# Joining the user tiles two weight blocks later in an embedding-mean projection

## The chip, the cores and the metric

The kernel runs on one core of one Trainium2 chip. The metric is the device time of one execution in microseconds (us). The profile is of one execution, and its times count from the start of its span.

## The reference

There are 1024 users with 200 ids each, a table of 12500 rows of 512 floats, and a projection of 512 by 12500 with a bias.

```
valid = sequence_ids < emb_table.shape[0]
seq_emb = emb_table[where(valid, ids, 0)] * valid
user_repr = seq_emb.sum(axis=1) / max(valid.sum(axis=1), 1)
logits = user_repr @ proj_w + proj_b
```

The ids are drawn up to 109962, so only about one in nine is valid. The kernel sorts each user's ids so that the valid ones stand first, and gathers the first 26 of them (FAST), one "column" of 128 rows at a time. Users that have more get a share called the rest.

## The kernel before

**Tiles and units.** The users are 8 tiles of 128. The projection's 12500 outputs are 25 blocks of 500 (BW). A *unit* is one tile times one block. In fp32 precision it takes 12 matmuls on TensorE (PE), four for each of high*high, high*low and low*high. There are 200 units, and a unit's number is `r`. While ScalarE (ACT) moves a unit out of PSUM (`by_act`), the bias is a thirteenth matmul (line 806). Where VectorE (DVE) moves it out (line 609), the bias is part of the move. Until unit `joined[1]` ACT moves all units, until `joined[5]` every second one (the even `r`), then DVE moves all.

**Weights.** A *load* q brings block q modulo 25 (1000 KB) by a DMA of the queue SP, line 283. ACT copies it to `w_hi` (line 416, `w_high`), DVE forms `w_lo` (lines 595 and 597, `w_low`). The split blocks stand in a ring of 5 (SPLIT). The raw loads stand in a ring of 4 up to load 15, since two buffers lie over the means of tiles 4 to 7, which are written later (`raw_at_hi`, `raw_at_lo`). From load 16 on (MORE_LOADS) the ring has the 2 buffers `w_raw`. SP asks for a load once `w_low` is done with the load that had its buffer before:

```
raw_slot = [q if q <= ONCE else (q - 1) % ONCE if q < MORE_LOADS else q % RAW for q in range(LOADS)]
split_due = [None] * SPLIT + [min(last_unit[q - SPLIT] + 1, first_unit[q] - 1) for q in range(SPLIT, LOADS)]
```

`split_due[q]` is the unit at which ACT and DVE split load q in their program order. ACT waits there for the load, and what stands behind it on ACT waits too.

**Means and joins.** The sum of a tile's 26 columns must be there before the tile's first unit, the tile's *join*. GpSimd (POOL) gathers the columns (line 347) into a ring of 12 (ROWS): gather c needs column c-11 to be used (c even). DVE adds most columns into `sums` (line 539). PE adds the last 8 of tile 1 and the last 2 of tile 2 into `turned` by diagonal matrices (line 757) that ACT builds (line 400, `diagonal`, a ring of 4). The steps of a join are: the rest's share (PE line 749, ACT line 433), the mean (DVE line 584), the turn (PE line 732), `mean_hi` (ACT line 422), `mean_lo` (DVE line 589). Between two joins DVE also sorts the next tile's ids (lines 478 to 496). I call the stretch from the turn of tile t-1 to the turn of tile t *stage t*.

**What sets the order.** The tuple JOIN gives the load at which each tile joins. A tile joins with the last four loads still in the ring of 5 and then takes part in each load for 25 blocks. From JOIN all lists above are computed at build time (`units`, `first_unit`, `last_unit`, `joined`, `split_due`, `column_due`), and each engine's program is one loop over `r` in which these lists say what stands where. DVE's columns of tile t are spread evenly from unit `joined[t-1] - 2` (0 for tile 1) to unit `joined[t] - 3`.

```
JOIN=(0, 10, 14, 17, 20, 22, 24, 26)
start = [max(0, q - (SPLIT - 1)) if t else 0 for t, q in enumerate(JOIN)]
```

On ACT, in the loop over `r`, the diagonals stand ahead of `w_high(q)` of the same `r`, and behind those of the units before:

```
for c in range(FAST, COLS):
    if by_pe[c] and column_due(c) == r + 1:
        diagonal(c)
for q in range(SPLIT, LOADS):
    if split_due[q] == r:
        w_high(q)
if by_act[r]:
    move_out(r)
```

Of the kernel before, what the change touches and what calls it, by code (L numbers as in the profile page):

```python
# [3 lines left out]


def mean_embedding_projection(nc, ids, table, proj, bias, out, FAST=26,
                              JOIN=(0, 10, 14, 17, 20, 22, 24, 26)):
    F32, F32R, BF16 = mybir.dt.float32, mybir.dt.float32r, mybir.dt.bfloat16
    I32, U32 = mybir.dt.int32, mybir.dt.uint32
    ALU, ACT, AX = mybir.AluOpType, mybir.ActivationFunctionType, mybir.AxisListType  # L10
# [38 lines left out]

    start = [max(0, q - (SPLIT - 1)) if t else 0 for t, q in enumerate(JOIN)]  # L50
    LOADS = start[-1] + NB
    steps = []
    for q in range(LOADS):
        for t in range(1, TILES):
            if JOIN[t] == q:
                steps += [(x, t, 1) for x in range(start[t], q)]
        here = [t for t in range(TILES) if JOIN[t] <= q < start[t] + NB]
        steps.append((q, here[0], len(here)))
# [41 lines left out]
    raw_last = [max((x for x in range(q) if raw_slot[x] == raw_slot[q]), default=None) for q in range(LOADS)]  # L100
    assert MORE_LOADS < JOIN[TILES // 2] and RAW_AT + BW <= (STAGE - K) * BW

# [728 lines left out]
```

## Time and profile before

| | |
|---|---|
| median of 3 executions | 642.86 us (642.55 to 642.87) |
| the profiled execution | 643.35 us |
| its span | 641.6 us |
| PE busy | 609.1 us (95%) |
| DVE busy | 407.9 us (64%) |
| POOL busy | 233.6 us (36%) |
| ACT busy | 137.6 us (21%) |
| joins (first unit of tiles 1 to 7) | 10, 22, 35, 51, 65, 81, 98 |
| loads | 47 |

PE is busy nearly throughout, so what counts is each gap on PE and what ended it. A busy share of another engine is to be read by stage: DVE has 64% over the span, but the means are all formed in the first 357 us.

### The profile page before, as it was taken

How to read it: one execution, taken by the hardware profiler on the slowest of the kernel's cores; microseconds unless marked ns; L12 is line 12 of the kernel's file. 1: busy time of each engine (PE TensorE's matmuls, PEld its weight loads, DVE VectorE, ACT ScalarE, POOL GpSimd, SP SyncE). 2: the span in 40 equal slices, each digit the busy share in tenths (PEclk: the TensorE clock that was granted, in tenths of full speed). 3: DMA queues.
4: the chain of work that ended last, by engine and by line, in shares of the span. 5: the costliest groups of instructions: out<-in, count | busy, mean ns of one | idle time of the engine just before them, and what ended most of it. 6: DMA issues, size and time to landing. Idle time of an engine off the chain costs nothing.

```text
span 641.6 us, 7583 instructions
## 1 busy us (share of the span) xinstructions
PE 609.1 (95%) x2602; PEld 476.1 (74%) x2602; DVE 407.9 (64%) x723; ACT 137.6 (21%) x153; POOL 233.6 (36%) x227
## 2 busy tenths in 40 slices
PE   1878799989999999999999999999999999999997
PEld 0326558777778787788788788888888888888886
DVE  7977958989878898697786454333333333344442
ACT  7605426132122131300200221110011111211210
POOL 5777777777764767566550000000000000000000
PEclk9999989999999999999999999999999999999999
DMA  9979999999998999798793398454555555566632
GB/s 311 388 259 331 380 390 293 373 329 318 315 296 298 305 291 313 236 323 249 236 341 121 97 288 260 127 173 161 177 176 177 176 177 176 171 185 201 223 127 103
DMA packets 77703, 158.31 MB, mean 247 GB/s; under 512 B 9287, under 2 KB 65042, under 8 KB 77658
## 3 DMA queue, kind: packets, MB, share of 16 engines
q1 hardware_dynamic: 60378, 110.30, 50.7%
q0 software_dynamic: 17280, 47.47, 23.2%
q8 instruction: 21, 0.34, 0.2%
q14 instruction: 24, 0.20, 0.1%
HBM read 115.70 MB, written 51.20 MB: 260 GB/s over the span
## 4 chain that ended last, share of the span: by engine, by line
PE 75%; DVE 13%; DMA 6%; issue 5%; ACT 1%; DVEq 1%; POOL 0%; POOLq 0%; ACTq 0%
PE acc L801 70%; DVE sums L539 5%; DMA rows<-in_L_rec_emb_table_dram,index 4%; PE turned L757 2%; DMA w_raw<-in_L_rec_proj_w_dram 2%; DVE w_lo L597 2%; DVE key L496 1%; DVE w_lo L595 1%; DVE top L492 1%; PE acc L806 1%; ACT w_hi L416 1%; DVE stage L609 1%; PE turned L749 1%; DVE mean L584 0%; PE turned L732 0%
## 5 line engine op out<-in xcount | busy, mean ns | idle before, releaser
L347 POOL DMA_INDIRECT rows<-in_L_rec_emb_table_dram,index x208 | 224.1, 1077 | 95.7 <-issue 58.1
L801 PE MATMUL acc<-w_hi,mean_hi 128*128 128x500 f32 x800 | 224.4, 402 | 0.8 <-ACT mean_hi L422 0.8
L609 DVE TENSOR_TENSOR stage<-acc,bias_sb 128x500 f32<-128x500 f32 x162 | 109.3, 676 | 179.4 <-PE acc L801 179.3
L801 PE MATMUL acc<-w_hi,mean_lo 128*128 128x500 f32 x800 | 213.8, 389 | 0.3 <-DVE mean_lo L589 0.3
L801 PE MATMUL acc<-w_lo,mean_hi 128*128 128x500 f32 x800 | 214.0, 389 | 0.0
L801 PEld LDWEIGHTS acc<-w_hi,mean_lo 128*128 128x128 f32 x800 | 150.1, 188 | 32.4 <-DVE mean_lo L589 1.6
L801 PEld LDWEIGHTS acc<-w_hi,mean_hi 128*128 128x128 f32 x800 | 150.2, 189 | 31.9 <-issue 4.3
L801 PEld LDWEIGHTS acc<-w_lo,mean_hi 128*128 128x128 f32 x800 | 150.2, 188 | 31.3
L539 DVE SCALAR_TENSOR_TENSOR sums<-rows,mask,sums 128x512 f32<-128x512 f32 x165 | 124.1, 752 | 8.8 <-DMA rows<-in_L_rec_emb_table_dram,index 0.6
L416 ACT ACTIVATE w_hi<-w_raw 128x2000 fp32r<-128x2000 f32 x39 | 72.9, 1875 | 236.3 <-PE acc L801 215.7
L595 DVE TENSOR_TENSOR w_lo<-w_raw,w_hi 128x1000 fp32r<-128x1000 f32 x39 | 46.5, 1193 | 13.4 <-ACT w_hi L416 13.3
L597 DVE TENSOR_TENSOR w_lo<-w_raw,w_hi 128x1000 fp32r<-128x1000 f32 x39 | 46.6, 1196 | 0.0
L407 ACT ACTIVATE stage<-acc 128x500 f32<-128x500 f32 x38 | 22.2, 586 | 79.9 <-PE acc L806 79.9
L433 ACT ACTIVATE rest_mean<-turned,inv_count 128x512 f32<-128x512 f32 x7 | 4.8, 690 | 76.3 <-PE turned L749 68.9
L757 PE MATMUL turned<-rows,diags_at_hi 128*128 128x512 f32 x30 | 15.8, 663 | 3.1 <-DMA rows<-in_L_rec_emb_table_dram,index 3.1
L492 DVE MAX8 top<-key 128x8 f32<-128x200 f32 x40 | 14.6, 366 | 0.7
L757 PEld LDWEIGHTS turned<-rows,diags_at_hi 128*128 128x128 f32 x30 | 5.8, 210 | 12.4 <-DMA rows<-in_L_rec_emb_table_dram,index 7.2
L757 PE MATMUL turned<-rows,diag 128*128 128x512 f32 x20 | 11.2, 698 | 3.9 <-ACT diag L400 3.7
L806 PE MATMUL acc<-bias_parts,pick 89*128 89x500 bf16 x38 | 14.6, 385 | 0.0
L422 ACT ACTIVATE mean_hi<-turned 128x512 fp32r<-128x512 f32 x8 | 4.8, 598 | 45.4 <-PE turned L732 45.4
L584 DVE SCALAR_TENSOR_TENSOR mean<-sums,inv_count,rest_mean 128x512 f32<-128x512 f32 x7 | 5.3, 751 | 14.0 <-issue 6.9
L496 DVE MATCH_REPLACE8 key<-top,key 128x200 f32<-128x200 f32 x40 | 14.1, 352 | 0.0
(106 smaller groups left out, 180.9 us busy)
## 6 DMA issues: line engine op xcount, KB each, us to landing
out_dram<-stage SPq DMA_DIRECT2D x200, 250.0 KB, 3.8
w_raw<-in_L_rec_proj_w_dram SPq DMA_DIRECT2D x39, 1000.0 KB, 6.6
bias_sb<-in_L_rec_proj_b_dram SPq DMA_DIRECT2D x39, 250.0 KB, 4.9
raw_at_hi<-in_L_rec_proj_w_dram SPq DMA_DIRECT2D x4, 1000.0 KB, 11.1
rows<-in_L_rec_emb_table_dram,index POOLq DMA_INDIRECT x208, 5.8
raw_at_lo<-in_L_rec_proj_w_dram SPq DMA_DIRECT2D x3, 1000.0 KB, 13.7
stage<-in_L_rec_proj_w_dram SPq DMA_DIRECT2D x1, 1000.0 KB, 23.8
ids_sb<-in_r_sequence_ids_dram SPq DMA_DIRECT2D x1, 700.0 KB, 4.4
```

The source lines that it names most:

```text
L347: return pool.indirect_dma_start(out=dst, out_offset=None, in_=table, in_offset=bass.IndirectOffsetOnAxis(ap=column, axis=0), bounds_check ...
L407: nc.scalar.activation(stage[:, g % STAGE, r - stores[g][0]], acc[:, r % BANKS, 0:BW], ACT.Copy).then_inc(s_moved_by_act, 1)
L416: nc.scalar.activation(w_hi[:, q % SPLIT], raw(q), ACT.Copy).then_inc(s_w_hi, 1)
L492: dve.max(eight, key[:]).then_inc(s_sort, 1)
L496: dve.match_replace(key[:], eight, key[:], -1.0).then_inc(s_sort, 1)
L539: dve.scalar_tensor_tensor(sums[:], rows[:, c % ROWS], mask[:, t, j:j + 1], sums[:], ALU.mult, ALU.add).then_inc(s_summed, 1)
L595: dve.tensor_tensor(w_lo[:, q % SPLIT, 0:half], raw(q)[:, 0:half], w_hi[:, q % SPLIT, 0:half].bitcast(F32), ALU.subtract)
L597: dve.tensor_tensor(w_lo[:, q % SPLIT, half:], raw(q)[:, half:], w_hi[:, q % SPLIT, half:].bitcast(F32), ALU.subtract).then_inc(s_w_lo, 1)
L609: dve.tensor_tensor(stage[:, g % STAGE, r - stores[g][0]], acc[:, r % BANKS, 0:BW], bias_sb[:, i % BIAS], ALU.add).then_inc(s_moved_by_dve, 1)
L757: nc.tensor.matmul(turned[:], diagonal_of(c), rows[:, c % ROWS], start=j == 0, stop=j == FAST - 1).then_inc(s_added, 1)
L801: last = nc.tensor.matmul(bank, first, second, start=part + k == 0, stop=part == 2 and k == K - 1 and not by_act[r])
L806: last = nc.tensor.matmul(bank, pick[:, q % NB:q % NB + 1].to_broadcast([BIAS_ROWS, P]), bias_parts[:], start=False, stop=True)
```

## The change

Every tile from the second on joins two loads later. The kernel's text changes in one line:

```
-                              JOIN=(0, 10, 14, 17, 20, 22, 24, 26)):
+                              JOIN=(0, 12, 16, 19, 22, 24, 26, 28)):
```

Worked out from the lists: tile 0 takes 12 loads alone instead of 10. The joins stand at units 12, 24, 37, 53, 67, 82 and 98. There are 49 loads instead of 47, and still 200 units. ACT moves out 40 units instead of 38, so two more bias matmuls run. From unit 98 on each unit's place in the program is the same, with each load's number two higher. MORE_LOADS stays at 16, ON_PE (which columns PE adds) stays as it is. In stage 3 the loads split are 17, 18 and 19 (at units 25, 26, 27) instead of 15, 16 and 17 (at 23, 24, 25). In stage 2 they are 13 to 16 instead of 11 to 14. Ahead of tile 1's join, up to the unit before the diagonals, they run to load 12 instead of load 10.

**ScalarE ahead of the join of tile 1.** The rows are of the difference on ACT, from the split of load 10 on; `raw_at_hi` and `raw_at_lo` are loads 11 and 12.

```order
 L416 ACTIVATE w_hi<-w_raw 128x2000
 L407 ACTIVATE stage<-acc 128x500
+L416 ACTIVATE w_hi<-raw_at_hi 128x2000
+L407 ACTIVATE stage<-acc 128x500
+L416 ACTIVATE w_hi<-raw_at_lo 128x2000
+L407 ACTIVATE stage<-acc 128x500
 L400 ACTIVATE diag<-ident,mask 128x128 x8
 L407 ACTIVATE stage<-acc 128x500
```

The splits of loads 11 and 12, each with a wait for its load, now stand ahead of the eight diagonals instead of behind the join.

**TensorE at the same place.** The rows are of the difference on PE, from the end of unit 7 on.

```order
 L801 MATMUL acc<-w_hi,mean_lo 128x500 x4
 L806 MATMUL acc<-bias_parts,pick 128x500
+L801 MATMUL acc<-w_hi,mean_hi 128x500 x4
+L801 MATMUL acc<-w_lo,mean_hi 128x500 x4
+L801 MATMUL acc<-w_hi,mean_lo 128x500 x4
+L806 MATMUL acc<-bias_parts,pick 128x500
+L801 MATMUL acc<-w_hi,mean_hi 128x500 x4
+L801 MATMUL acc<-w_lo,mean_hi 128x500 x4
+L801 MATMUL acc<-w_hi,mean_lo 128x500 x4
+L806 MATMUL acc<-bias_parts,pick 128x500
 L749 MATMUL turned<-rest_rows,placed 128x512
 L757 MATMUL turned<-rows,diag 128x512 x8
```

Two units, 8 and 9, now run ahead of PE's eight columns instead of behind them.

**VectorE in stage 3.** The rows are of the difference on DVE, at the first of the three splits in stage 3.

```order
 L539 SCALAR_TENSOR_TENSOR sums<-rows,mask,sums 128x512
 L609 TENSOR_TENSOR stage<-acc,bias_sb 128x500
-L595 TENSOR_TENSOR w_lo<-raw_at_hi,w_hi 128x1000
-L597 TENSOR_TENSOR w_lo<-raw_at_hi,w_hi 128x1000
+L595 TENSOR_TENSOR w_lo<-w_raw,w_hi 128x1000
+L597 TENSOR_TENSOR w_lo<-w_raw,w_hi 128x1000
 L539 SCALAR_TENSOR_TENSOR sums<-rows,mask,sums 128x512 x2
 L595 TENSOR_TENSOR w_lo<-w_raw,w_hi 128x1000
```

The order of the work is the same, but the first split now reads one of the two `w_raw` buffers, so all three loads of the stage share two buffers. The third, load 19, can only be asked for when the first, load 17, is split.

## Rows read from the trace of the kernel before

**Rows 1.** The page, busy time of each engine.

```profile
PE 609.1 (95%) x2602; PEld 476.1 (74%) x2602; DVE 407.9 (64%) x723; ACT 137.6 (21%) x153; POOL 233.6 (36%) x227
```

**Rows 2.** Windows by stage (2, 3, 4): length, busy of each engine, clock, DMA share.

```profile
92.60:132.30 39.70, 37.97 (x168) 29.27 (x166) 35.81 (x68) 13.81 (x17) 30.57 (x29) 1.00 0.98 343
132.30:171.70 39.40, 39.00 (x174) 30.67 (x174) 36.65 (x71) 10.28 (x12) 28.47 (x29) 1.00 0.95 316
171.70:218.90 47.20, 47.20 (x212) 37.50 (x213) 38.17 (x72) 11.38 (x14) 29.78 (x28) 1.00 0.91 300
```

**Rows 3.** Timeline of TensorE: start, length, instruction, idle before and releaser.

```profile
75.61 1.02 PE L749 MATMUL turned<-rest_rows,placed 128*128 128x512 f32 x2
80.36 9.51 PE L757 MATMUL turned<-rows,diag 128*128 128x512 f32 x16 [3.73 <-ACT diag L400]
...
132.26 0.66 PE L732 MATMUL turned<-ident,mean 128*128 128x128 f32 x4 [1.73 <-DVE mean L584]
...
171.68 0.66 PE L732 MATMUL turned<-ident,mean 128*128 128x128 f32 x4 [0.36 <-DVE mean L584]
```

**Rows 4.** Windows of 1 us at two gaps of TensorE; the eighth number is PEclk.

```profile
81.00:82.00 1.00, 1.00 (x2) 0.34 (x1) 1.00 (x2) 0.09 (x1) 0.69 (x2) 0.50 1.04 387
...
84.00:85.00 1.00, 1.00 (x3) 0.41 (x3) 0.56 (x1) 0.51 (x2) 0.70 (x2) 1.00 1.05 401
...
131.00:132.00 1.00, 0.00 (x0) 0.00 (x0) 0.55 (x1) 0.22 (x1) 0.70 (x2) 1.00 1.01 360
```

**Rows 5.** Chain that ended last, 64 to 93 us: start, length, what.

```profile
64.45 12.75 DMA w_raw<-in_L_rec_proj_w_dram
...
77.58 1.88 ACT w_hi L416
...
79.48 0.04 DVE w_lo L595
...
83.16 5.53 DMA rows<-in_L_rec_emb_table_dram,index
...
89.87 2.71 PE acc L801 x12
92.57 0.23 PE acc L806
```

**Rows 6.** Timeline of ScalarE, the first four diagonals of tile 1.

```profile
79.82 1.26 ACT L400 ACTIVATE diag<-ident,mask 128x128 f32<-128x128 f32 x4
```

**Rows 7.** Timeline of the queue SP: requests of loads 12 and 15.

```profile
72.79 0.39 SPq L283 DMA_DIRECT2D raw_at_lo<-in_L_rec_proj_w_dram  x1
...
105.39 0.39 SPq L283 DMA_DIRECT2D raw_at_hi<-in_L_rec_proj_w_dram  x1
```

**Rows 8.** Line 283 in the window 72.7 to 73 us (load 12).

```profile
DMA to landing us min/median/max: 13.7/13.7/13.7
```

**Rows 9.** Line 283 in the window 105 to 105.6 us (load 15).

```profile
DMA to landing us min/median/max: 9.2/9.2/9.2
```

**Rows 10.** Line 283 in the window 149 to 149.4 us (load 18).

```profile
DMA to landing us min/median/max: 8.9/8.9/8.9
```

**Rows 11.** Timeline of VectorE in stage 2: end of split 11, start of split 14.

```profile
104.17 1.19 DVE L597 TENSOR_TENSOR w_lo<-raw_at_hi,w_hi 128x1000 fp32r<-128x1000 f32 x1
...
115.61 1.19 DVE L595 TENSOR_TENSOR w_lo<-w_raw,w_hi 128x1000 fp32r<-128x1000 f32 x1
```

**Rows 12.** Timeline of VectorE in stage 3: end of split 15, start of split 17.

```profile
144.21 1.19 DVE L597 TENSOR_TENSOR w_lo<-raw_at_hi,w_hi 128x1000 fp32r<-128x1000 f32 x1
...
151.90 1.19 DVE L595 TENSOR_TENSOR w_lo<-w_raw,w_hi 128x1000 fp32r<-128x1000 f32 x1
```

**Rows 13.** Timeline of VectorE in stage 4: end of split 18, start of split 20.

```profile
182.85 1.19 DVE L597 TENSOR_TENSOR w_lo<-w_raw,w_hi 128x1000 fp32r<-128x1000 f32 x1
...
194.50 1.20 DVE L595 TENSOR_TENSOR w_lo<-w_raw,w_hi 128x1000 fp32r<-128x1000 f32 x1 [3.87 <-ACT w_hi L416]
```

**Rows 14.** Waits in stage 6 (260.7 to 308 us): total, times, longest.

```profile
DVE stage L609 <- PE acc L801: 6.3, 5, 2.2
```

## The prediction

> **What bounds the kernel now.** I read the page's busy times first: PE is busy 609.1 of 641.6 us [rows 1], so the work on PE is the floor and the rest is gaps. Then I listed PE's timeline for idle time and its releaser. After the first unit there are few gaps, and all stand at joins: the largest is ahead of tile 1's columns (3.73 us, until ACT's diagonals), then 1.73 us at tile 2's turn and 0.36 us at tile 3's, both until DVE's mean [rows 3]. The third view, busy time by stage, says who sets each stage. In stage 2 DVE is busy 35.81 of 39.70 us and in stage 3 36.65 of 39.40 us [rows 2]. With its small gaps between dependent operations, that is a full engine, and PE waits for it at the end of both stages. So a microsecond added to DVE in stage 2 or 3 is a microsecond of PE idle. In stage 6 DVE waits 6.3 us for PE's products [rows 14], so there it has room.
>
> The gap at tile 1 has a cause of its own. The chain that ended last goes through the transfer of load 10 (12.75 us), then its copy to `w_hi` at 77.58 us, and only then come the diagonals [rows 5, 6]. ACT stood in its queue at the split of load 10, with the diagonals behind it. PE's columns then run from 80.36 to 89.87 us. Eight columns are 16 matmul rows; at full clock one column takes 0.86 us (6.9 us in all), and the rest is two columns at half clock (1.7 us more; the granted clock is 0.50 at 81 us and 1.00 again at 84 us [rows 4], the lower and the upper of the two levels) and the gather that lands at 88.69 us [rows 5].
>
> **The change part by part.**
>
> *Bias matmuls.* ACT moves two more units, so PE runs two more bias matmuls of 0.23 us [rows 5]: +0.5 us. DVE has two moves fewer, but they fall outside stages 2 and 3, whose share of moves and splits is the same as before.
>
> *Tile 1's join.* Units 8 and 9 now run ahead of the columns. By themselves they would fill the gap: unit 7 ends at 75.6 us [rows 3], two units with bias take 2 x 2.95 = 5.9 us (12 matmuls in 2.71 us and 0.23 us of bias [rows 5]), so PE is ready for its columns at 82.4 us with the rest's 0.86 us. But on ACT the splits of loads 11 and 12 now stand ahead of the diagonals, and each waits for its load. Load 12 is asked for at 72.79 us and lands 13.7 us later, at 86.5 us [rows 7, 8]. From the landing to `w_hi` is 0.38 us (load 10: 64.45 + 12.75 = 77.20, then 77.58), from the start of that copy to the first diagonal 2.24 us (77.58 to 79.82), from there to PE's first column 0.54 us [rows 3, 5, 6]. So the columns start at 86.5 + 0.38 + 2.24 + 0.54 = 89.7 us and PE idles 7 us instead of 3.7. With two columns at half clock again they take 8.6 us and end at 98.2 us, against 89.87 us before. Of these 8.3 us 5.9 are units done, so 2.4 us are lost. DVE adds two columns (1.5 us) fewer ahead of split 8, so load 12 is asked for up to 1.5 us earlier. The DMA engines are full there (share 1.04 [rows 4]), so I credit half of it: **+1.7 us**. The bounds are 0 (an earlier landing by 2.4 us) and 4 (a second stretch at half clock).
>
> *Stage 2.* DVE's order relative to the join is as before, moved by two units, but the loads are 13 to 16. Load 16 takes the buffer of load 13, so it is asked for when DVE has split 13, the place where split 11 stood. Before, that split ended at 105.36 us, and a load asked for at 105.39 us landed 9.2 us later [rows 7, 9, 11]. From landing to the start of DVE's split is 2.28 us by load 10 (77.20 to 79.48 us [rows 5]). So the fourth split could start at 105.39 + 9.2 + 2.28 = 116.9 us, where it stood at 115.61 us [rows 11], 1.3 us later. Another row gives less: in stage 4 of the kernel before, load 20 waits in the same way for split 18, and from the end of that split (184.04 us) to the start of split 20 (194.50 us) are 10.5 us, with 3.87 us of idle on DVE [rows 13]. By that the split starts at 115.8 us, 0.2 us later. Between the two I stand nearer to the first, whose landing is of this very place: **+1.0 us** of DVE wait, in a stage that DVE sets. Bounds: 0.2 and 1.3 us.
>
> *Stage 3.* This is the large term. The loads are 17, 18, 19 in two buffers. Load 19 is asked for at the end of split 17, where split 15 ended at 145.40 us. Load 18, the nearest row in this stage, landed after 8.9 us [rows 10]. So split 19 would start at 145.43 + 8.9 + 2.28 = 156.6 us where split 17 started at 151.90 us [rows 12], 4.7 us later. By stage 4's 10.5 us it would be 155.9 us, 4.0 us later. I take **+4.5 us**. In stage 4 that wait cost PE nothing (busy 47.20 of 47.20 us [rows 2]), but the stage has 16 units; stage 3 has 13, and PE waited at its end already. Behind DVE's wait stand its columns, and behind these POOL, whose ring of 12 rows is full. ACT's copy for load 19 holds back its moves by some 5 us, but a PSUM bank is used again only six units later (17 us), so PE does not wait for them. Bounds: 4.0 us, and 5.0 us with load 15's 9.2 us to landing [rows 9].
>
> *Clock.* PE's gap at the turn of tile 3 grows from 0.36 to 4.9 us. The gap ahead of tile 1's columns cost 1.7 us in clock, that of 1.73 us at tile 2 cost nothing (PEclk 1.00 [rows 4]). The new gap is longer than the first, but one row is little evidence: bounds 0 and 1.7 us, I take **+0.9 us**. For stage 2's gap of 2.7 us I take nothing, bounds 0 and 1.7.
>
> *Stages 4 to 7 and the tail.* Stages 4 and 5 keep their length in units and their splits' buffers. Stages 6 and 7 are one unit shorter (15 and 16). That takes 2.7 us from DVE's time in stage 6 and one of its moves from its work, and it has 6.3 us of waits for products to give: 0. From unit 98 on nothing moves.
>
> The sum is 0.5 + 1.7 + 1.0 + 4.5 + 0.9 = 8.6 us. On the profiled execution's 643.35 us that gives 651.95 us. The median of the runs is 0.49 us below it, so I predict **651.5 us**.
>
> **A rule against it.** A load of 1000 KB took 8.9 to 13.7 us from request to landing [rows 8 to 10]. The Trainium skill (DMA: Bandwidth & Descriptors, Anatomy of one DMA) gives a fit of 2.0 us plus bytes over 436 GB/s, measured on GpSimd's path, which by estimate is 4.35 us for such a load. By that the wait in stage 3 would be 4.35 + 2.28 - 6.5 = 0.1 us (6.5 us lie between the end of split 15 and the start of split 17), and those ahead of the diagonals and in stage 2 would be gone too. The trace disagrees: beside gathers and stores, at DMA shares of 0.95 to 1.04, the same transfer takes two to three times as long.
>
> **The rivals.**
> 1. *Quick loads (faster).* If loads landed fast, the two solo units would fill PE's gap at tile 1. The last row of the tile (landed at 88.69 us, and up to 1.5 us later since DVE frees its slot later) would then end the columns at about 91.2 us, against 95.8 us (89.87 + 5.9): -4.6 us. This needs load 12 within 8.4 us of its request. Stage 3 costs the landing time less 4.2 us. Both together win only if landings fall below about 8 us; at 4.4 us the result is 643.35 - 4.6 + 0.5 - 0.5 = 638.8 us. For it: the gap is there to be filled. Against it: 13.7 us at load 12 [rows 8]. This is what the page's fit would give.
> 2. *DVE makes the wait good.* If stage 3's 4.5 us are regained before the mean, that term and the clock's vanish: 651.5 - 5.4 = 646.1 us. For it: stage 4 did so before. Against it: 36.65 of 39.40 us busy [rows 2].
> 3. *Slow loads.* If load 19 takes as long as load 12 (13.7 us), stage 3 costs 9.5 us: about 656.5 us. Against it: the DMA share there is 0.95 and the neighbours took 8.9 us.
> 4. *Nothing moves but places.* Each join keeps its wait, only two units later: 642.9 + 0.5, within the noise of this case at 643.3 us. Against it: the buffers' ring does not move with the joins.
>
> **How the numbers follow.** Forecast 80%, rival 2 7%, rival 3 5%, rival 1 4%, rival 4 4%. The forecast's own range is its terms' bounds, 0.5 + 0 + 0.2 + 4.0 + 0 = 4.7 us to 0.5 + 4 + 1.3 + 5.0 + 3.4 = 14.2 us; not all ends meet, so 648 to 655.5 us. Down to 646 us it takes in rival 2. The range is 646.0 to 655.5 us. A change of 0.2% (1.3 us) is about what a measurement of this kernel can tell from none: faster 4% (rival 1), same 4% (rival 4), slower 92%.
>
> **What the changed profile would show.** PE's gap ahead of tile 1's columns is near 7 us, with ACT's copies of loads 11 and 12 just ahead of the first diagonal. DVE waits about 1 us at its fourth split in stage 2 and about 4.5 us at its third in stage 3, and ACT waits there for `w_raw`. PE's waits at the turns of tiles 2 and 3 are near 2.7 and 4.9 us, those of tiles 4 to 7 as before. A clock of 0.50 behind tile 3's turn settles the clock term. The prediction is wrong if load 12 lands before 81 us, if load 19 lands within 5 us, or if PE does not wait at tile 3's turn.

## The result: 1.8% slower

| | before | changed |
|---|---|---|
| median | 642.70 us (641.76 to 642.87) | 654.73 us (652.88 to 655.1) |
| profiled execution | 643.35 us | 652.88 us |
| its span | 641.6 us | 651.1 us |
| PE busy | 609.1 us | 612.1 us |
| loads | 47 | 49 |

The ratio is 1.0184 with a 95% interval of 1.0163 to 1.0206, so the change costs 12.0 us. The first profiled execution is the quickest of these four runs of the changed kernel, 9.5 us above its counterpart. A second one (below, the changed kernel again) took 655.5 us and shows where the rest is.

The page of the changed kernel, busy time of each engine, which answers to [rows 1]. PE is busy 3.0 us longer: 0.5 us are the two bias matmuls, most of the rest is the same work at half clock. The other 6.5 us of the 9.5 us are idle time.

```profile
PE 612.1 (94%) x2604; PEld 478.0 (73%) x2604; DVE 410.9 (63%) x725; ACT 142.4 (22%) x157; POOL 231.9 (36%) x227
```

The timeline of TensorE of the changed kernel answers to [rows 3]. The gap ahead of tile 1's columns grew from 3.73 to 6.35 us, that at tile 2's turn fell from 1.73 to 1.51 us, and that at tile 3's turn grew from 0.36 to 4.54 us. The four matmuls that begin at 185.00 us take 1.98 us, the four at 188.44 us 1.09 us.

```profile
81.85 1.02 PE L749 MATMUL turned<-rest_rows,placed 128*128 128x512 f32 x2
89.22 8.92 PE L757 MATMUL turned<-rows,diag 128*128 128x512 f32 x16 [6.35 <-ACT diag L400]
...
141.07 0.66 PE L732 MATMUL turned<-ident,mean 128*128 128x128 f32 x4 [1.51 <-DVE mean L584]
...
184.58 0.72 PE L732 MATMUL turned<-ident,mean 128*128 128x128 f32 x4 [4.54 <-DVE mean L584]
185.00 1.98 PE L801 MATMUL acc<-w_hi,mean_hi 128*128 128x500 f32 x4
...
188.44 1.09 PE L801 MATMUL acc<-w_hi,mean_lo 128*128 128x500 f32 x4
```

Windows of 1 us of the changed kernel, the clock being the number ahead of the DMA share, answer to [rows 4]. Behind both long gaps PE ran at the lower level, 0.50: at 90 us in tile 1's columns and at 187 us behind the turn of tile 3. At the second place, the start of stage 4, the kernel before had a mean of 1.00 over the whole stage [rows 2].

```profile
90.00:91.00 1.00, 1.00 (x2) 0.33 (x1) 1.00 (x2) 0.00 (x0) 0.69 (x2) 0.50 1.06 389
...
187.00:188.00 1.00, 1.00 (x3) 0.76 (x3) 0.90 (x4) 0.00 (x0) 0.96 (x1) 0.50 0.79 306
```

The timeline of ScalarE of the changed kernel answers to [rows 6]. The copies of loads 11 and 12 stand ahead of the diagonals, each behind a wait of 2 us for its transfer, and the first diagonal starts at 88.68 us instead of 79.82 us.

```profile
81.98 1.87 ACT L416 ACTIVATE w_hi<-raw_at_hi 128x2000 fp32r<-128x2000 f32 x1 [2.05 <-DMA raw_at_hi<-in_L_rec_proj_w_dram]
...
86.44 1.87 ACT L416 ACTIVATE w_hi<-raw_at_lo 128x2000 fp32r<-128x2000 f32 x1 [2.11 <-DMA raw_at_lo<-in_L_rec_proj_w_dram]
...
88.68 1.26 ACT L400 ACTIVATE diag<-ident,mask 128x128 f32<-128x128 f32 x4
```

Line 283 of the changed kernel in the window 69 to 73 us, load 12, answers to [rows 8]; it was asked for at 71.7 us, 1.1 us earlier than before.

```profile
DMA to landing us min/median/max: 14.7/14.7/14.7
```

The timeline of VectorE of the changed kernel, the fourth split of stage 2 and the first and third of stage 3, answers to [rows 11, 12]. From the end of split 17 (154.20 us) to the start of split 19 are 10.4 us, where the same places were 6.5 us apart.

```profile
124.42 1.20 DVE L595 TENSOR_TENSOR w_lo<-w_raw,w_hi 128x1000 fp32r<-128x1000 f32 x1 [0.47 <-ACT w_hi L416]
...
153.01 1.19 DVE L597 TENSOR_TENSOR w_lo<-w_raw,w_hi 128x1000 fp32r<-128x1000 f32 x1
...
164.63 1.20 DVE L595 TENSOR_TENSOR w_lo<-w_raw,w_hi 128x1000 fp32r<-128x1000 f32 x1 [3.85 <-ACT w_hi L416]
```

Windows by stage of the changed kernel (stages 2, 3 and 4) answer to [rows 2]. Stage 3 took 43.5 us instead of 39.4 with the same 36.7 us of DVE work; stage 2 is half a microsecond longer. In stage 4 the mean clock is 0.96.

```profile
101.00:141.50 40.50, 38.54 (x172) 29.48 (x170) 36.08 (x69) 13.69 (x17) 28.36 (x27) 1.00 0.94 311
141.50:185.00 43.50, 38.90 (x177) 30.62 (x174) 36.74 (x71) 10.28 (x12) 28.82 (x28) 1.00 0.95 311
185.00:230.00 45.00, 45.00 (x195) 35.78 (x193) 37.03 (x71) 10.84 (x13) 27.93 (x27) 0.96 0.91 293
```

The starts of the turns (line 732 on PE) give the whole account:

| turn of tile | before | changed | stage before | stage changed |
|---|---|---|---|---|
| 1 | 92.64 | 100.92 | | |
| 2 | 132.26 | 141.07 | 39.62 | 40.15 |
| 3 | 171.68 | 184.58 | 39.42 | 43.51 |
| 4 | 218.90 | 233.44 | 47.22 | 48.86 |
| 5 | 260.66 | 275.26 | 41.76 | 41.82 |
| 6 | 308.02 | 319.90 | 47.36 | 44.64 |
| 7 | 357.11 | 366.63 | 49.09 | 46.73 |

Tile 1's turn is 8.3 us later, of which 5.9 us are two more units done and 0.4 us lie ahead of the first unit. Stages 6 and 7 are each one unit shorter and give 5.1 us of this back. A unit is 2.7 us, so 0.3 us are missing, and they are in stage 7 (49.09 - 46.73 = 2.4 us).

### The profile page after: what moved, and what is told of

The parts are those of the page before. It is cut to its first block, busy times and chain, and to the rows that moved or that the text cites. A ratio compares the mean times of both kernels' runs of the same rounds, so it can differ in the third digit from the quotient of the medians.

```text
span 651.1 us, 7598 instructions
## 1 busy us (share of the span) xinstructions
PE 612.1 (94%) x2604; PEld 478.0 (73%) x2604; DVE 410.9 (63%) x725; ACT 142.4 (22%) x157; POOL 231.9 (36%) x227
## 4 chain that ended last, share of the span: by engine, by line
PE 79%; DVE 8%; DMA 7%; issue 3%; ACT 1%; DVEq 1%; POOL 0%; POOLq 0%; ACTq 0%
PE acc L801 73%; PE turned L757 4%; DVE sums L539 3%; DMA rows<-in_L_rec_emb_table_dram,index 3%; DMA raw_at_lo<-in_L_rec_proj_w_dram 2%; DMA w_raw<-in_L_rec_proj_w_dram 1%; DVE w_lo L597 1%; ACT w_hi L416 1%; PE acc L806 1%; DVE key L496 1%; PE turned L749 1%; DVE top L492 1%; PE turned L732 1%; DVE mean L584 0%; DVEq L253 0%
## 5 line engine op out<-in xcount | busy, mean ns | idle before, releaser
L609 DVE TENSOR_TENSOR stage<-acc,bias_sb 128x500 f32<-128x500 f32 x160 | 107.8, 676 | 179.0 <-PE acc L801 178.9
L416 ACT ACTIVATE w_hi<-w_raw 128x2000 fp32r<-128x2000 f32 x41 | 76.5, 1877 | 249.1 <-PE acc L801 209.2
L595 DVE TENSOR_TENSOR w_lo<-w_raw,w_hi 128x1000 fp32r<-128x1000 f32 x41 | 48.9, 1193 | 17.7 <-ACT w_hi L416 17.6
L597 DVE TENSOR_TENSOR w_lo<-w_raw,w_hi 128x1000 fp32r<-128x1000 f32 x41 | 49.0, 1195 | 0.0
L757 PE MATMUL turned<-rows,diag 128*128 128x512 f32 x20 | 11.1, 702 | 6.8 <-ACT diag L400 6.3
L757 PEld LDWEIGHTS turned<-rows,diag 128*128 128x128 f32 x20 | 4.2, 226 | 13.5 <-issue 11.6
## 6 DMA issues: line engine op xcount, KB each, us to landing
raw_at_lo<-in_L_rec_proj_w_dram SPq DMA_DIRECT2D x3, 1000.0 KB, 14.7
```

The costliest lines, as they stand in the source:

```text
L416: nc.scalar.activation(w_hi[:, q % SPLIT], raw(q), ACT.Copy).then_inc(s_w_hi, 1)
L595: dve.tensor_tensor(w_lo[:, q % SPLIT, 0:half], raw(q)[:, 0:half], w_hi[:, q % SPLIT, 0:half].bitcast(F32), ALU.subtract)
L597: dve.tensor_tensor(w_lo[:, q % SPLIT, half:], raw(q)[:, half:], w_hi[:, q % SPLIT, half:].bitcast(F32), ALU.subtract).then_inc(s_w_lo, 1)
L609: dve.tensor_tensor(stage[:, g % STAGE, r - stores[g][0]], acc[:, r % BANKS, 0:BW], bias_sb[:, i % BIAS], ALU.add).then_inc(s_moved_by_dve, 1)
L757: nc.tensor.matmul(turned[:], diagonal_of(c), rows[:, c % ROWS], start=j == 0, stop=j == FAST - 1).then_inc(s_added, 1)
```

## The experiments

Times within one group were taken on the same chip, beside the kernel before. Since its median differs from group to group by up to 0.8 us, the differences to it are compared: the changed kernel has +12.0 us.

**First group** (kernel before: 642.76 us). *Four raw buffers up to load 19*, in the changed kernel:

```
-    RAW_MORE, MORE_LOADS = 2, 16
+    RAW_MORE, MORE_LOADS = 2, 20
```

> The changed kernel with the ring of four raw buffers kept up to load 19 (MORE_LOADS 20 instead of 16), so that loads 16 to 19 are asked for long before their split. Theory (the two-buffer ring is the largest part of the loss): VectorE's waits of 0.5 us in stage 2 and 3.9 us in stage 3 go, TensorE's gap at tile 3's turn falls from 4.5 us to about 0.4 us and its clock does not fall there (1.7 us), so about 648.5 us against 654.7 us of the changed kernel. Rival (VectorE's wait was regained, the loss is all at tile 1's join): within 1 us of 654.7 us.

Measured: 646.16 us, ratio 1.0051 (1.0034 to 1.0068), +3.4 us. The waits for loads in stages 2 and 3 are gone, and tile 3's turn waits 0.38 us, as in the kernel before. TensorE's timeline of this kernel:

```profile
88.75 8.94 PE L757 MATMUL turned<-rows,diag 128*128 128x512 f32 x16 [6.22 <-ACT diag L400]
...
179.44 0.66 PE L732 MATMUL turned<-ident,mean 128*128 128x128 f32 x4 [0.38 <-DVE mean L584]
```

The buffers are worth 8.6 us of the 12.0 us, more than the 6.2 us I expected: the expectation was made from the quick profile. The theory stands; its rival, that VectorE regains its wait, is out. Stage 2 is 39.5 us long here (140.01 - 100.47), so the wait of 0.47 us at its fourth split had cost about as much in the changed kernel (40.15 us). What is left is tile 1's gap of 6.2 us.

*The two-buffer ring one load earlier in the kernel before*, joins untouched:

```
-    RAW_MORE, MORE_LOADS = 2, 16
+    RAW_MORE, MORE_LOADS = 2, 15
```

> The kernel before with the ring of four raw buffers up to load 14 only (MORE_LOADS 15 instead of 16), joins untouched: load 17 then waits for the split of load 15 in stage 3, as load 19 does for 17 in the changed kernel. Theory: this alone brings the stage 3 loss back, VectorE waits some 4 us at the third split of stage 3, TensorE's gap at tile 3's turn grows from 0.4 to some 4.4 us, with or without 1.7 us of half clock: 646.8 to 648.8 us against 642.7 us. Rival (the wait is harmless in the old order, the joins do the damage): within 1 us of 642.7 us.

Measured: 650.23 us, ratio 1.0109 (1.009 to 1.0129), +7.5 us. It brings the loss of stage 3 into the old order, so the loss belongs to the ring and not to the joins. VectorE's timeline of this kernel (end of split 15, start of split 17), then TensorE's at tile 3's turn:

```profile
143.20 1.19 DVE L597 TENSOR_TENSOR w_lo<-w_raw,w_hi 128x1000 fp32r<-128x1000 f32 x1
...
155.94 1.20 DVE L595 TENSOR_TENSOR w_lo<-w_raw,w_hi 128x1000 fp32r<-128x1000 f32 x1 [4.97 <-ACT w_hi L416]
```

```profile
175.94 1.11 PE L732 MATMUL turned<-ident,mean 128*128 128x128 f32 x4 [5.63 <-DVE mean L584]
```

DVE waits 5.0 us, since load 17 took 9.5 us to land. Stage 3 is 5.3 us longer (175.94 - 131.27 = 44.7 us) and stage 4, which begins at half clock, 2.6 us longer (49.8 us). The loss of 7.5 us is above my range of 4.1 to 6.1 us by 1.4 us: the wait was 1 us longer than the 4 us that I took, and the half clock cost 2.6 us and not 1.7. The edit also moves the request of load 15 (it now waits for the split of 14), but no wait in stage 2 came of it.

*Early diagonals in the changed kernel:*

```
-    ON_PE, DIAGS = ((0, FAST), (18, FAST), (24, FAST)), 4
+    ON_PE, DIAGS = ((0, FAST), (18, FAST), (24, FAST)), 8
-    GROUP, STAGE = 1, 11
+    GROUP, STAGE = 1, 10
-                    if by_pe[c] and column_due(c) == r + 1:
+                    if by_pe[c] and column_due(c) == r + (3 if c < 2 * FAST else 1):
```

> The changed kernel with tile 1's eight diagonals built ahead of the split of load 11 on ScalarE, in a ring of 8 diagonals (the room is taken from the output stage, 10 slots instead of 11). Theory (at tile 1's join TensorE waits for diagonals queued behind loads 11 and 12): the columns start near 83 us instead of 89.2 us and end when the tile's last row has landed, near 91.5 us instead of 98.2 us; about 6.5 us less, 648 us. Rival (the gathers, or units 10 and 11 which need their splits, take over at once): the columns end no earlier than 96 us, and at most 2 us are gained.

Measured: 650.11 us, ratio 1.0114 (1.009 to 1.0139), +7.4 us, a gain of 4.6 us, where I had expected 6.5. TensorE's timeline of this kernel: the columns start at 82.43 us, in step, and end at 90.78 us, not at 98.14 us.

```profile
82.43 4.70 PE L757 MATMUL turned<-rows,diag 128*128 128x512 f32 x10
87.43 3.35 PE L757 MATMUL turned<-rows,diag 128*128 128x512 f32 x6 [0.30 <-DMA rows<-in_L_rec_emb_table_dram,index]
...
100.38 1.17 PE L801 MATMUL acc<-w_hi,mean_lo 128*128 128x500 f32 x4 [1.22 <-DVE mean_lo L589]
...
130.82 2.23 PE L757 MATMUL turned<-rows,diag 128*128 128x512 f32 x4 [2.31 <-DMA rows<-in_L_rec_emb_table_dram,index]
```

At tile 1's turn 7.2 us are gained (93.77 against 100.92 us), as the theory says, and then part of it is given back: stage 2 takes 42.05 us instead of 40.15. PE waits 1.22 us for `mean_lo` and 2.31 us for gathered rows of tile 2. In the window of stage 2 of this kernel POOL issues 31 gathers instead of the 27 of the changed kernel. GpSimd issues one every 1.3 us (1.0 us and 0.3 us between), as its timeline shows first, and never pauses for longer than 0.3 us in the stage. So 31 of them are 40 us of the 42:

```profile
95.09 1.00 POOL L347 DMA_INDIRECT rows<-in_L_rec_emb_table_dram,index  x1 [0.31 <-issue]
96.40 1.00 POOL L347 DMA_INDIRECT rows<-in_L_rec_emb_table_dram,index  x1 [0.30 <-issue]
...
93.80:135.80 42.00, 38.47 (x166) 29.13 (x167) 37.45 (x70) 13.21 (x16) 32.85 (x31) 1.00 0.98 345
```

*Early diagonals in the kernel before*, the same edit with `r + 2`:

> The kernel before with the same edit: tile 1's eight diagonals ahead of the split of load 10, ring of 8 diagonals, 10 output slots. Theory: the 3.7 us wait for the diagonals goes, but the columns still end with the last row, which lands at 88.7 us, so the time stays within 1 us of 642.7 us. Rival (the wait that the profile names is the loss): 3.7 us and the 1.7 us of half clock are gained, about 637.5 us.

Measured: 642.82 us, ratio 0.9996 (0.9985 to 1.0006): nothing that the medians show. (In its one profile tile 1's turn stands at 91.25 us, 1.4 us earlier than in the profile of the kernel before, but the interval leaves room for less than 1 us.) The wait that the profile names first, 3.7 us for the diagonals, can be taken away and the time stays, since the row behind it is as late. TensorE's timeline of this kernel shows the same columns in pieces, each waiting for its gather, with the last ending at 88.47 us:

```profile
76.65 1.12 PE L757 MATMUL turned<-rows,diag 128*128 128x512 f32 x2 [0.16 <-DMA rows<-in_L_rec_emb_table_dram,index]
79.18 2.19 PE L757 MATMUL turned<-rows,diag 128*128 128x512 f32 x4 [1.41 <-DMA rows<-in_L_rec_emb_table_dram,index]
82.17 1.13 PE L757 MATMUL turned<-rows,diag 128*128 128x512 f32 x2 [0.80 <-DMA rows<-in_L_rec_emb_table_dram,index]
84.19 4.28 PE L757 MATMUL turned<-rows,diag 128*128 128x512 f32 x8 [0.90 <-DMA rows<-in_L_rec_emb_table_dram,index]
```

**Second group** (kernel before: 643.45 us). *Both edits in the changed kernel* (MORE_LOADS 20, and the three lines of the early diagonals):

> The changed kernel with both edits: the ring of four raw buffers up to load 19, and tile 1's diagonals ahead of the split of load 11 (ring of 8, 10 output slots). Theory (two separate losses that add): 654.7 - 8.6 (measured for the buffers alone) - 4.6 (measured for the diagonals alone) = 641.5 us, with TensorE's gaps at the turns of tiles 2 and 3 at 1.7 us and less, so at or a little under the kernel before (642.8 us). Rival (the gains overlap, since stage 2's sums are late when tile 1's join is early): 644 to 646 us.

Measured: 643.50 us, ratio 1.0001 (0.9989 to 1.0013). The two edits together undo the whole loss, 11.6 us in this group (655.13 us for the changed kernel, below), but are 1.6 us short of the sum of 8.6 and 4.6 us, so the time lies between my two expectations. The window of stage 2 of this kernel, and below it that of the kernel with the buffers alone, differ by 4 us: 32 gathers instead of 27, and DMA share 1.01 instead of 0.96. Some 2 us of these are waits for rows and for `mean_lo`, as with the early diagonals alone, where they are counted in the 4.6 us already. Another 1.6 us are new: the mean clock is 0.96. The granted clock was 0.50 from 133.8 to 137.2 us, behind a wait of 1.86 us for a row, while with the early diagonals alone it stayed at 1.00 behind 2.31 us. That is about what the sum is short of, but it is one profile.

```profile
95.70:139.20 43.50, 40.07 (x168) 30.00 (x167) 38.36 (x72) 13.24 (x16) 34.05 (x32) 0.96 1.01 359
```

```profile
100.50:140.00 39.50, 38.04 (x167) 29.18 (x165) 35.65 (x68) 13.82 (x17) 28.95 (x27) 1.00 0.96 328
```

*The changed kernel again, unedited:*

> The changed kernel once more, unedited, for a second profile and more times. Theory (the spread between its runs, 652.9 to 655.1 us, comes from TensorE's half clock behind its two long gaps): in this profile the sum of half clock and time go together, 10.2 us of half clock at 652.9 us and 3.4 us more of it at 654.6 us and above. Rival (the spread comes from the transfers): the half clock is the same as in the first profile while the gaps at tile 1's columns or at tile 3's turn differ by 2 us.

Measured: 655.13 us, ratio 1.0177 (1.0155 to 1.02), +11.7 us; the profiled execution took 655.5 us. TensorE's timeline of it, then line 283 for load 12 (asked for at 71.4 us), then VectorE at split 19:

```profile
89.82 9.73 PE L757 MATMUL turned<-rows,diag 128*128 128x512 f32 x16 [7.41 <-ACT diag L400]
...
187.19 1.12 PE L732 MATMUL turned<-ident,mean 128*128 128x128 f32 x4 [5.92 <-DVE mean L584]
```

```profile
DMA to landing us min/median/max: 15.6/15.6/15.6
```

```profile
167.25 1.20 DVE L595 TENSOR_TENSOR w_lo<-w_raw,w_hi 128x1000 fp32r<-128x1000 f32 x1 [5.25 <-ACT w_hi L416]
```

Both of my readings hold in part. The transfers were slower (load 12 took 15.6 us instead of 14.7, load 19 9.8 us instead of 8.4), and the half clock lasted longer in the columns: they took 9.73 us instead of 8.92. Behind tile 3's turn it cost the same as in the first profile (stage 4 took 48.86 us in both), though the gap was 1.4 us longer. Over the ten executions of the changed kernel the mean granted clock and the time go together: 0.990 to 0.992 in the three up to 654.1 us, 0.984 to 0.989 in the seven from 654.6 us on. This fits the theory but doesn't decide, since a longer gap holds more idle time at the lower level too. Tile 1's turn came 1.4 us later than in the first profile and tile 3's 1.2 us more.

*Relief in stage 3 alone.* The changed kernel; load 16 still waits for the split of 13, load 19 takes the buffer of load 12:

```
-    raw_slot = [q if q <= ONCE else (q - 1) % ONCE if q < MORE_LOADS else q % RAW for q in range(LOADS)]
+    raw_slot = [q if q <= ONCE else (q - 1) % ONCE if q < 16 else q - 16 if q < MORE_LOADS else q % RAW for q in range(LOADS)]
```

with MORE_LOADS 20.

> The changed kernel with the four raw buffers kept for loads 16 to 19 in another order, so that load 16 still waits for the split of 13 as in the changed kernel, but load 19 no longer for the split of 17. Theory (nearly all of the buffers' part is stage 3): VectorE's wait of 0.5 us in stage 2 stays, that in stage 3 goes, and the time is within 1 us of the 646.2 us with all waits gone. Rival (stage 2's wait is worth more in the other runs than in the profile): 648 us or more.

Measured: 648.63 us, ratio 1.0074 (1.0057 to 1.0092), +5.2 us, so 1.8 us more than with all waits gone, and neither expectation is met cleanly: the time is that of the rival, the profile is that of the theory. In its profile DVE's wait in stage 2 is 0.32 us and PE's at tile 3's turn 0.42 us. Stage 2 took 40.1 us against 39.5 us, and tile 1's turn came 3.2 us later (103.66 against 100.47 us). Stage 3's relief is thus worth 6.5 to 6.8 us. Whether the 1.8 us is stage 2's wait or tile 1's join can't be told from one profile each: this kernel asks for load 16 five units later, and its first join was among the late ones. The columns of tile 1 began 2.2 us later (90.97 against 88.75 us), and up to there the two programs are the same, so in the profiles at least this part is spread between executions and not the edit.

*Tile 1 stays*, the kernel before with

```
-                              JOIN=(0, 10, 14, 17, 20, 22, 24, 26)):
+                              JOIN=(0, 10, 16, 19, 22, 24, 26, 28)):
```

> One part of the change alone: tiles 2 to 7 join two loads later, tile 1 stays at load 10. Joins at units 10, 26, 39, 55, 69, 84, 100. Theory: tile 1's columns keep the timing of the kernel before (the 2 us lost there come back), stage 2 has 16 units instead of 12 so its 1.5 us gap goes, and stage 3 keeps the wait for load 19: 642.8 + 0.5 - 1.6 + 4.1 + 1.7 to 3.4 = 647.5 to 649.2 us. Rival (every later join costs as the whole change does): near 654.7 us.

Measured: 648.14 us, ratio 1.0071 (1.0049 to 1.0092), +4.7 us, as expected. Tile 1's turn is back at 91.54 us and tile 2's has no gap, but stage 3 keeps its wait. In the profiled execution (649.84 us, one of the longer ones) it is larger than the 4.1 us expected: load 19 took 11.1 us and stage 3 45.8 us, 6.4 us more than before. The timeline of TensorE at tile 3's turn:

```profile
186.44 1.12 PE L732 MATMUL turned<-ident,mean 128*128 128x128 f32 x4 [7.22 <-DVE mean L584]
```

**Third group** (kernel before: 643.13 us). *Tile 1 stays, and four raw buffers up to load 19:*

> Tiles 2 to 7 join two loads later, tile 1 stays at load 10, and the four raw buffers are kept up to load 19. Theory: both losses of the changed kernel are gone, and with 16 units in stage 2 its gap of 1.6 us goes too, at the price of two bias matmuls (0.5 us): 1.1 us under the kernel before, about 641.6 to 642.4 us beside 642.8 to 643.4 us. Rival (the six splits of stage 2 fill VectorE, so the gap moves to tile 3's turn): the same time as the kernel before or up to 2 us above.

Measured: 641.09 us, ratio 0.997 (0.9959 to 0.9982). This beats the kernel before by 2.0 us, a little more than expected. At the turns of tiles 2 and 3 TensorE's timeline has no gap any more, and behind tile 3's there is one of 0.30 us. Those at tiles 6 and 7 stay (0.79 and 0.74 us, before 1.04 and 0.73):

```profile
141.04 0.60 PE L732 MATMUL turned<-ident,mean 128*128 128x128 f32 x4
...
185.48 1.18 PE L801 MATMUL acc<-w_hi,mean_lo 128*128 128x500 f32 x4 [0.30 <-DVE mean_lo L589]
...
313.55 0.66 PE L732 MATMUL turned<-ident,mean 128*128 128x128 f32 x4 [0.79 <-DVE mean L584]
```

*The same with the joins 15, 18, 21, 23, 25, 27 for tiles 2 to 7:*

> As the one before with tiles 2 to 7 joining one load later instead of two (14 units in stage 2 instead of 12 or 16). Theory: stage 2's gap of 1.6 us needs only half of the room, so the same gain with one bias matmul less, 1.3 us under the kernel before. Rival (stage 2 gains no room, since splits come with the units): within 0.6 us of the kernel before.

Measured: 641.08 us, ratio 0.997 (0.9958 to 0.9981): the same gain with half of the shift. Stage 2's two more units are enough: tile 2's turn has no gap here either. The old joins with more buffers were not run, but in the kernel before no split of stages 2 and 3 waited for its load, so there was nothing in them for more buffers to give.

## Why the prediction was right, step by step

The direction and the places were right, and the time was within the range (651.5 us forecast, 654.7 us measured, range 646.0 to 655.5 us). The size was short: 12.0 us measured against 8.8 forecast, 0.8 us inside the upper end of the range. That the forecast sum nearly meets the first profile is partly luck, since this is one of the quickest executions of the changed kernel; the second is nearer to the median. The terms, from the turns of the two profiles of the changed kernel (the first 9.5 us above the kernel before in span, the second 12.2 us):

| term | forecast | first profile | second profile |
|---|---|---|---|
| bias matmuls | 0.5 | 0.5 | 0.5 |
| tile 1's join | 1.7 | 2.4 | 3.8 |
| stage 2 | 1.0 | 0.5 | 0.3 |
| stage 3 | 4.5 | 4.1 | 5.5 |
| clock behind tile 3's turn | 0.9 | 1.6 | 1.6 |
| sum | 8.6 | 9.1 | 11.7 |

The measured entries are differences of turns less two biased units (tile 1) or of stage lengths; the remaining 0.4 to 0.5 us lie in stages 5 to 7, nearly all in stage 7, and the tail.

- **What bounds the kernel.** That DVE sets stages 2 and 3 held: 3.85 us of wait in a stage with 36.74 us of work came out as 4.1 us of stage. The ring in the old order did the same (4.97 and 5.3 us). The list of gaps was incomplete: it left out those at the turns of tiles 6 and 7, 1.04 and 0.73 us, both until DVE's mean.
- **Tile 1's join** was the term mis-sized. The mechanism was right, diagonals behind the splits of loads 11 and 12, and removing it gave 7.2 us at the turn. But the step "I credit half of it", for the earlier request of load 12, failed. The request came 1.1 to 1.4 us earlier, and the landing came at 86.4 and 87.0 us where it had come at 86.5. Without the credit the working gave 2.4 us; the first profile has 2.0 us and 0.4 us from ahead of the first unit. In the second profile the term is 3.8 us: load 12 landed 0.5 us later than before, and the half clock cost 0.8 us more in the columns than in the first, which I had only as a bound.
- **Stage 2** was too high. The split waited 0.47 and 0.27 us, near the lower of my two rows (0.2 us). The gap at tile 2's turn did not grow to 2.7 us: it was 1.51 and 1.16 us, with waits of 0.45 and 0.61 us for a gathered row ahead of it. I chose the row of the same place over the row of the same pattern; load 16 landed after 8.8 and 8.6 us, not 9.2.
- **Stage 3** was right in size and range by the first profile, and 0.5 us above the range's 5.0 us in the second, where load 19 took 9.8 us to land.
- **Clock.** The half clock came behind the gap of 4.5 us, and behind 5.6 and 5.9 us in the others. For the changed kernel the row that I halved (1.7 us) was the right one; behind the 5.6 us of the ring in the old order it was 2.6 us.
- **Stages 4 to 7.** No new gap came with one unit less in stages 6 and 7, whose lengths fell by 2.7 and 2.4 us, but the two that were there grew, from 1.04 to 1.26 and from 0.73 to 1.10 us. The term of 0 was 0.3 us short in stage 7. The lines are TensorE's, of the kernel before and then of the changed kernel:

```profile
308.02 0.66 PE L732 MATMUL turned<-ident,mean 128*128 128x128 f32 x4 [1.04 <-DVE mean L584]
357.11 0.66 PE L732 MATMUL turned<-ident,mean 128*128 128x128 f32 x4 [0.73 <-DVE mean L584]
...
319.90 0.66 PE L732 MATMUL turned<-ident,mean 128*128 128x128 f32 x4 [1.26 <-DVE mean L584]
366.63 0.66 PE L732 MATMUL turned<-ident,mean 128*128 128x128 f32 x4 [1.10 <-DVE mean L584]
```

Of the rivals, the quick loads fell: loads 12, 16 and 19, on which the terms rest, took 8.4 us and more in both profiles. The fit of the Trainium skill (DMA: Bandwidth & Descriptors, Anatomy of one DMA) gives 4.35 us by estimate; the traces don't agree, since no load of the kernel before landed in under 5.1 us. That DVE makes the wait good is refuted by both kernels with the ring edited. Why did the same wait cost nothing in stage 4? It has 16 units to hide it in instead of 13, which is my explanation; no run tests it. The slow loads fell short of 13.7 us: load 19 took 8.4 and 9.8 us, and 11.1 us in one experiment.

## What to carry to other kernels

When a schedule's table is shifted, list what does not shift with it: here the number up to which loads have four buffers instead of two, a constant beside the table, and worth 8.6 of the 12.0 us. With that constant moved too, and tile 1 left where it was, later joins made the kernel 0.3% faster than before. Then look for waits in program order: work that is ready (the diagonals) behind work that waits for a transfer. And a wait named in the profile is not a gain until what is late next is known: the same edit gave 4.6 us in one kernel and nothing in the other.

## What the runs showed of the hardware

- **A request 1.2 us earlier brought nothing where the DMA engines were full.** Load 12 was asked for at 72.8, 71.7 and 71.4 us in three executions and took 13.7, 14.7 and 15.6 us, landing at 86.5, 86.4 and 87.0 us. It is the same over all twelve profiles: in the six in which tile 1 joins at load 10 it was asked for at 72.9 us in the mean and landed at 86.7, in the six in which it joins at load 12 at 71.7 and 86.8 us. The DMA share there is 1.02 to 1.06. Loads 10 and 11, asked for ahead of it, had not landed yet; whether they or the other transfers hold it back no run shows.
- **The half clock costs 1.7 to 2.9 us, and the length of the gap alone does not set it.** PE's eight columns took 8.92 us behind 6.35 us of idle and 9.73 us behind 7.41 us. But behind the gaps at tile 3's turn of 4.54, 5.63 and 5.92 us (the changed kernel, the ring in the old order, the changed kernel again) PE worked 3.4, 5.7 and 3.5 us at 0.50. It costs half of such a stretch. Gaps of 2.3 to 3.0 us ahead of tile 1's columns left the clock at 1.00 in four experiments, while in the kernel with both edits it fell behind one of 1.86 us. In the second profile of the changed kernel the granted clock, in the windows below, was still 0.50 at 94 us, more than four microseconds after the columns had begun:

```profile
92.00:93.00 1.00, 1.00 (x2) 0.34 (x1) 0.90 (x2) 0.31 (x1) 0.61 (x1) 0.50 1.14 423
94.00:95.00 1.00, 1.00 (x2) 0.34 (x1) 0.00 (x0) 0.01 (x1) 0.96 (x1) 0.50 0.95 349
95.00:96.00 1.00, 1.00 (x4) 0.45 (x3) 0.00 (x0) 0.40 (x1) 0.74 (x1) 0.95 0.81 241
```

- **GpSimd's gathers have a pace.** One column of 128 rows is issued every 1.3 us in these traces, and now and then one takes 2 us, so 31 of them fill a 42 us stage. Ending tile 1's join 7 us earlier takes the lead that POOL had, and stage 2 grows by 1.9 us, as waits for rows and for `mean_lo`.
